# Local attention on one core: probabilities times values in 64x32 tiles, one head at a time, instead of 64x128 tiles for two heads

## What is computed

```
HEADS, DIM_HEAD, WINDOW = 16, 64, 32
bk2, bv2 = look(bk), look(bv)          # this window's 32 keys and the 32 before it
sim = einsum('bhwie,bhwje->bhwij', bq, bk2) * 8.0
attn = softmax(where(mask, -max, sim), -1)
out = einsum('bhwij,bhwje->bhwie', attn, bv2)
```

## Time and profile before

| | |
|---|---|
| median of 3 runs | 4446.24 us (4435.07 to 4448.33) |
| the profiled execution | 4434.56 us, of which the span is 4432.8 us |
| busy: PE | 3666.4 us (83% of the span) |
| busy: PE weight loads | 2787.7 us (63%) |
| busy: DVE / ACT / POOL | 2661.7 / 2213.7 / 1684.8 us |
| instructions traced | 118638, of them 48264 matmuls and 48456 weight loads |

### The profile page before, as it was taken

The page is one execution under the profiler, slowest core; times in us unless marked ns, Lnnn a source line. Parts: engine busy times, 40 slices in busy tenths (PEclk is TensorE's granted clock), DMA queues, the critical chain, the costliest instruction groups (busy, mean ns, idle before and its releaser), DMA issues. The chain is left out here.

```text
span 4432.8 us, 118638 instructions
## 1 busy us (share of the span) xinstructions
PE 3666.4 (83%) x48264; PEld 2787.7 (63%) x48456; DVE 2661.7 (60%) x4159; ACT 2213.7 (50%) x4350; POOL 1684.8 (38%) x1564
## 2 busy tenths in 40 slices
PE   4665759989979988988998996789999765667998
PEld 1223448858858867867876883577777751226555
DVE  5985567537727727736745754655655256894554
ACT  4443347647747746746755754344444314441222
POOL 2652047517607706725734742132222213560000
PEclk7988979999999999999999998788788777996999
DMA  0000011101101101101101100000000000001000
GB/s 14 0 0 17 1 46 33 39 20 34 45 15 31 34 19 41 33 24 35 34 29 30 32 21 4 7 6 7 6 6 7 3 12 0 0 0 58 0 0 9
DMA packets 56552, 83.19 MB, mean 19 GB/s; under 512 B 13146, under 2 KB 32628, under 8 KB 54900
## 3 DMA queue, kind: packets, MB, share of 16 engines
q1 hardware_dynamic: 56052, 75.99, 5.7%
HBM read 30.87 MB, written 1.05 MB: 7 GB/s over the span
## 5 line engine op out<-in xcount | busy, mean ns | idle before, releaser
L1850 POOL TENSOR_TENSOR local_rot<-local_term 128x512 f32<-128x512 f32 x384 | 478.7, 1267 | 643.9 <-DVE local_term L2168 643.9
L2168 DVE TENSOR_TENSOR local_term<-bank,local_table 128x512 f32<-128x512 f32 x768 | 485.2, 675 | 108.2 <-ACT local_sq L2056 99.7
L2091 ACT ACTIVATE local_attn<-bank 64x256 f32<-64x256 f32 x768 | 291.2, 379 | 340.3 <-PE bank L1947 333.5
L272 POOL TENSOR_TENSOR mamba_hc<-mamba_state,mamba_c_all 128x512 f32<-128x512 f32 x256 | 319.6, 1269 | 310.1 <-DVE mamba_state L451 304.8
L1856 POOL TENSOR_TENSOR local_rot<-local_rot,local_inv 128x512 f32<-128x512 f32 x384 | 392.8, 1044 | 93.9 <-ACT local_inv L2067 92.5
L1891 PE MATMUL bank<-local_w_layer,local_xs 128*128 128x256 f32 x1536 | 399.3, 405 | 27.5 <-issue 19.3
L1891 PEld LDWEIGHTS bank<-local_w_layer,local_xs 128*128 128x128 f32 x1536 | 286.9, 197 | 80.8 <-issue 31.2
L2229 DVE TENSOR_REDUCE local_most<-bank 128x8 f32<-128x512 f32 x192 | 132.8, 692 | 310.4 <-PE bank L1926 310.4
L1947 PE MATMUL bank<-local_pt,local_v_moved 64*128 64x64 f32 x3072 | 314.9, 283 | 0.0
L1947 PE MATMUL bank<-local_pt,local_v_at 64*128 64x64 f32 x3072 | 305.7, 277 | 0.0
L451 DVE TENSOR_TENSOR_SCAN mamba_state<-bank,mamba_dbu 128x512 f32<-128x512 f32 x256 | 300.3, 1222 | 0.0
(11 more groups left out here) (367 smaller groups left out, 8202.8 us busy)
## 6 DMA issues: line engine op xcount, KB each, us to landing
local_v_moved<-local_v_at SPq DMA_DIRECT2D x192, 192.0 KB, 2.4
local_w_layer<-a_w_layer_dram SPq DMA_DIRECT2D x6, 1536.0 KB, 7.1
local_v_moved<-local_v_at SPq DMA_DIRECT2D x192, 32.0 KB, 2.0
moe_w<-f_w_dram SPq DMA_DIRECT2D x3, 2048.0 KB, 16.1
local_w_o<-a_w_o_dram SPq DMA_DIRECT2D x12, 256.0 KB, 3.8
local_w_up<-a_w_up_dram SPq DMA_DIRECT2D x6, 341.0 KB, 4.4
moe_w<-f_w_dram SPq DMA_DIRECT2D x3, 576.0 KB, 4.8
delta_w_h<-g_w_qkv_dram SPq DMA_DIRECT2D x8, 192.0 KB, 2.2
```

The source lines that it names most:

```text
L272: ins = pool.tensor_tensor(hc[:, b, h, :], state[:, b, h, :], c_all[:, b, :], ALU.mult)
L1850: pool.tensor_tensor(rot[:, i % 2, :, f, :], here[:, :, f, :], there[:, :, 1 - f, :], ALU.add).then_inc(summed, 1)
L2091: ins = act.activation(tokens[ch, v, :, :].rearrange("p k (r q) -> p k r q", r=2), g.bank[6 + v][ch, :].rearrange("p (k r h q) -> p k r h ...
L2168: dve.tensor_tensor(term[:, which, b, :], g.bank[b][:, :], table[:, which, :, :].rearrange("p n c -> p (n c)"), ALU.mult).then_inc(roped, 1)
```

## The change

`weigh_values` writes each window's product as four matmuls, one for each 32 channels, and each with only the 32 query columns of the head to which these channels belong. The stationary operand is 64 keys by 32 channels, the moving one 64 keys by 32 queries. The number of matmuls of a slot goes from 16 to 64, the unused halves are gone, and the results of v lie dense in the first 256 columns of bank 6 + v. `copy_out` becomes two activations of 128 partitions by 256 elements. The wait for `o_copied` is followed by a semaphore increment of its own (`wait_apart`).

```diff
@@ weigh_values
                 pe.wait_ge(v_shifted, s * 32 + 32)
-                pe.wait_ge(o_copied, s + 1)
+                wait_apart(pe, o_copied, s + 1, pe_passed)
                 for k in range(TPG):
                     for r in range(2):
                         for v in range(2):
                             keys = slice(2 * W * v, 2 * W * (v + 1))
-                            column = (2 * k + r) * H * W
-                            mm = pe.matmul(g.bank[6 + v][:, column:column + H * W],
-                                           (v_at if r else v_moved)[keys, TPG * group_of(i) + k, :], pt[keys, k, r, :],
-                                           start=True, stop=True)
+                            column = (2 * k + r) * W
+                            for ch in range(0, P, W):
+                                mm = pe.matmul(g.bank[6 + v][ch:ch + W, column:column + W],
+                                               (v_at if r else v_moved)[keys, TPG * group_of(i) + k, ch:ch + W],
+                                               pt[keys, k, r, ch // E * W:(ch // E + 1) * W], start=True, stop=True)
                 mm.then_inc(o_ready, 1)
@@ copy_out
                 for v in range(2):
-                    for hh in range(H):
-                        ch = slice(E * hh, E * (hh + 1))
-                        ins = act.activation(tokens[ch, v, :, :].rearrange("p k (r q) -> p k r q", r=2),
-                                             g.bank[6 + v][ch, :].rearrange("p (k r h q) -> p k r h q", k=TPG, r=2, h=H)[:, :, :, hh, :],
-                                             ACT.Copy)
+                    ins = act.activation(tokens[:, v, :, :], g.bank[6 + v][:, 0:GROUP // 2].rearrange("p (k t) -> p k t", k=TPG), ACT.Copy)
                 ins.then_inc(o_copied, 1)
```

## The result

The changed kernel takes **4496.6 us** (median of 4 runs, 4480.58 to 4503.17) against 4444.98 us before (4 runs), a ratio of 1.0115, 95% interval 1.0083 to 1.0146: 1.15% slower. The forecast was 4476 us, 0.7% slower. The profiled execution took 4495.63 us with a span of 4493.9 us, 61.1 us more span than before.

The account below looks back on a forecast made before the run. PE was taken to bound each slot: 0.65 us gained in the burst, 0.84 lost to late packets, +35 us over 186 slots, less 5 at layers' ends; with 11.7 us from profile to median, 4476 us, range 4395 to 4540.

Parts of the forecast that it names:

- What bounds the kernel: In the local stack's slots of 7.56 us: PE's list sets the length; the next engine needs about 6 us.
- The burst: PE's small matmuls in a slot: 128 pairs at 8.6 ns, 1.29 us in place of 1.94, gaining 0.65 us.
- The rival built on that size: A start-to-start floor per matmul pair makes the burst 3.3 us, some +250 us, 4700 us in all; chance 2%.
- Packets: PE's instruction packets, 379 to about 523: at 3.80 us each, some come too late in a slot's dense stretch.
- The loss of 0.84 us per slot: PE's dense stretch: a late second packet in 0.60 of the slots, costing 1.4 us each.
- The 0.5 us taken off: From a late packet's 1.9 us: cover by instructions PE already holds and the 0.32 us pause ahead of L1926.
- The reading of one packet held ahead: From the delta rule's idle times: PE holds one packet ahead and asks for the next when that is entered.
- The clock: Rival: idle times lower the granted clock for the dense matmuls after them, +1 us a slot, 4660 us; chance 7%.
- ACT: Copying attention's result: two activations for four, 0.78 us for 1.55 a slot, worth nothing inside the slots.
- The layers' ends: Last copy before the projection in each of 6 layers: 0.8 us less each, about 5 us in all.
- Sum: Per slot 7.56 - 0.65 + 0.84 = 7.75 us, 0.19 more than before; over the kernel 4476 us, 0.7% slower.

Follow-up runs that it names:

- e4: The changed kernel with the copy as four activations of 64 partitions by 256 elements, as before the change: 4538.26 us, ratio 1.0233.
- e1: The changed kernel with each product as two matmuls of 64 keys by 64 channels, 32 matmuls a slot instead of 64: 4310.64 us, ratio 0.9716.
- e7: e1 with POOL's two rotary additions split by half of the group, so the first half starts after two of four products: 4261.01 us, ratio 0.9622.
- e2: e1 with 32 one-column matmuls a slot that nobody reads, added among the products, 443 records a slot: 5780.79 us, ratio 1.3035.
- e5: e1 with 32 unread one-column matmuls a slot in 64x32 tiles, in one block ahead of the products: 4511.84 us, ratio 1.0183.
- e6: e5 with 16 added matmuls a slot in place of 32, 379 records a slot: 4428.29 us, ratio 0.999.

## Why the prediction was right, and where it was off

- **What bounds the kernel**: right. PE's list set the slot before, and what PE got faster it kept wherever packets came in time: the slots from 1730.89 and from the same place in the other five layers take 6.92 to 6.93 us, where they took 7.56, predicted 6.91. One row was misread: the 0.32 us of "issue" ahead of L1926 is an idle time of the weight loads (PEld), not of PE's matmuls, which were idle for 7.56 - 7.42 = 0.14 us of the slot.
- **The burst**: 1.36 us with its end instead of the predicted 1.29. The 128 pairs start 9.7 ns apart (from 1731.91 to the last start at 1733.15), near the 8.6 ns of the 32x32 tiles and not the 14.1 ns of L1926. PE gained 0.58 us here, predicted 0.65. The floor of about 25 ns from start to start, which the Trainium skill states ("TensorE: Matmul & The Clock Gate", the section on the 56 ns gap), does not hold in this trace for matmuls in tiles: by an estimate from the page's figure it would make this burst 3.2 us. The rival built on that size was added up too low: 3.3 us is 1.55 us more than the 1.75 of before, not 1.3 to 1.4, so some 290 us and not 250.
- **Packets**: the count, 523, was exact. The loss of 0.84 us per slot was the term that decided, and it was the right mechanism. PE's idle time for "issue" between the slots of a layer is 153.4 us, over 186 slots **0.82 us**; that this is so near 0.84 is in part luck, because the split was off. Late packets were predicted in 0.60 of the slots at 1.4 us. The 161 idle times are 0.87 a slot, and they were shorter, 0.95 us each; only 85 slots have 1 us or more of it, 0.46 of them. The 0.5 us taken off rested in part on the misread 0.32. What failed of this term is the count of late packets: it took only two boundaries inside one dense stretch of 410 instructions for one. The slots at 1737.82 and 1745.74 pause one after the other, the first late in L1948, the second in L1926. A likely reason, not tested by itself, is that at 1.73 packets of 3.80 us a slot, 6.6 us in all, too little slack is left in a slot of 6.93 us for PE to catch up before the next one. The reading of one packet held ahead fits the landings only in part: behind 73 of the 130 pauses the next packet set out 1.0 to 1.5 us after PE had gone on, behind the other 57 later, and why is not worked out.
- **The clock**: it was a rival at 7%, with +1 us a slot. It came in a small measure. Of the nine slots over 9.5 us three are the first of a layer, which took 8.65 us at a lower clock before too, and cost 1.1 us each beyond the other layers' first slots; the other six cost some 2 us each. That is 15 us in all or 0.08 us a slot. It is part of the 20 us by which the kernel is slower than forecast.
- **ACT**: "worth nothing inside the slots" is not shown for the change. As e4 has it, the four short copies would cost 40 to 50 us more once packets are late. The prediction's argument, that ACT waits for PE right before, held only in the kernel before, where 7.56 us left 1.6 us of slack. So the two copies give some of their time back in this kernel, by a way that stays half open.
- **The layers' ends**: -2.1 us each and not -0.8. I had counted the shorter last copy alone. Two more bursts stand in this distance and got shorter, by some 0.7 us each, and a pause for "issue" that I had not counted, of 3.2 to 4.9 us, stands in each of the five distances (the first ends at 880.34). That the distance shrank in spite of it means that other parts gained more than the 0.8; I haven't worked out which. Over the five distances the difference is 6.5 us.
- **Sum**: 7.582 - 0.58 + 0.82 + 0.08 = 7.90 us, against 7.974 measured and 7.75 predicted; for the 0.07 left I have no term. Over all 186 slots PE's busy time fell by 0.42 us a slot and its idle time rose by 0.81. So what is missing is in PE's own time, which gained less on average than the 0.58 of an undisturbed burst less the 0.08 of the clock. The change was slower, for the reason given, and the time was inside the range.
- **What it missed**: it took the slot without late packets to be limited by PE alone. At 6.9 us another chain closes, over two slots, from the projection through ACT's squares, DVE's products and POOL's sums back to L1909 (e1, e7). It made no difference to this forecast, but it would have been the next limit if the packets had come in time.

## What to carry to other kernels

Count an engine's instructions beside its busy time: here PE can take some 255 instructions per 3.8 us, so, once the packet held ahead is used up, a stretch of small tiles that needs less time than that per 255 is bound by the program's own transfer, whatever the array can do. Make a tile as wide as it can be without computing something twice before making it narrower (64 keys by one head's 64 channels here: ratio 0.9716, against 1.0115 for half as wide). To test whether an engine's time or its instruction count costs, add the same time once as many short and once as few long instructions, in a place where the form of the tile changes no more often.

## What the runs showed of the hardware that I had not expected

- A change between 64x64 and 64x32 tiles costs PE about 0.15 us (e2). With 32 of them a slot and the same number of instructions and packets as e5, the slot took 14.3 us and not 8.0; 32 x 0.15 = 4.8 us of that are the changes by this estimate, and the granted clock fell too.
- In 64x64 tiles with 32 columns the pairs start 0.94 us/64 = 15 ns apart, in 64x32 tiles 9.7 ns. Per key, channel and query the wider tile is the cheaper one.
- Behind the pause of 1.56 us in the slot from 1833.34 the granted clock went down (0.83 over the slot), while the pauses of 0.67 and 0.83 us in the slots shown above left it at 1.00. It is not the length of a pause alone: pauses of 1.60, 1.56, 1.55 and 1.56 us, ending at 1790.87, 2165.48, 2197.20 and 2495.04, left it at 1.00. Nor is it the count: e6 has fewer pauses than the change (in 87 slots against 147) and more slots over 9.5 us (17 against 9). What decides it stays open.
